# Attention and mixture-of-experts kernel on one core: the down projection of the leading shared blocks read as one 512-column product, its halves added by VectorE

## What is computed

```
x = x + layernorm(attention(layernorm(x)))
x = x + layernorm(ffn(layernorm(x)))

def ffn(hidden, gate_w, Wg, Wu, Wd, Sg, Su, Sd):
    flat_x = hidden.reshape(8192, 256)
    scores = softmax(flat_x @ gate_w.T).T                   # 16 experts
    topk_weight, topk_idx = top_k(scores, 1024)
    xg = flat_x[topk_idx]
    h = gelu(xg @ Wg.T) * (xg @ Wu.T)                       # 1024 hidden columns per expert
    eo = (h @ Wd.T) * topk_weight
    flat_out = zeros.at[topk_idx].add(eo)
    shared = (gelu(hidden @ Sg.T) * (hidden @ Su.T)) @ Sd.T # 512 hidden columns
    return flat_out + shared
```

## Time and profile before

| | |
|---|---|
| median of 3 runs | 1948.2 us (1948.04 to 1949.56) |
| the profiled execution's own time | 1948.25 us |
| its span, first to last instruction | 1946.2 us |
| TensorE busy | 1919.5 us, 99% |
| VectorE busy | 1368.9 us, 70% |
| ScalarE busy | 1036.9 us, 53% |
| mean granted TensorE clock | 0.996 |
| front blocks in the span | about 585 to 804 us |

### The profile page before, as it was taken

One profiled execution on the slowest core, in us unless ns is written; L12 is line 12 of the kernel. 1 busy time (PEld: TensorE's weight loads), 2 busy tenths in 40 slices (PEclk: granted clock), 3 DMA queues, 4 the chain that ended last, 5 costly groups with the idle time before them and its releaser, 6 DMA issues.

```text
span 1946.2 us, 29069 instructions
## 1 busy us (share of the span) xinstructions
PE 1919.5 (99%) x10608; PEld 1647.2 (85%) x10608; DVE 1368.9 (70%) x2619; ACT 1036.9 (53%) x1929; POOL 521.9 (27%) x611
## 2 busy tenths in 40 slices
PE   8999999999999999999999999999999999999996
PEld 6888888888888888888888888888888888888886
DVE  6777787777776888767677777656565756565647
ACT  5457576675655445445454544545454545455455
POOL 0031132033030000322432333243234323432146
PEclk9999999999999999999999999999999999999998
DMA  3113323324244111444434443444434443434566
GB/s 131 55 33 101 86 100 109 97 78 139 52 157 155 66 61 43 136 82 104 92 89 106 94 99 81 107 87 110 87 97 99 91 105 92 105 85 107 152 216 173
DMA packets 153338, 197.37 MB, mean 101 GB/s; under 512 B 104449, under 2 KB 121089, under 8 KB 145153
## 3 DMA queue, kind: packets, MB, share of 16 engines
q1 hardware_dynamic: 127824, 158.00, 26.1%
q0 software_dynamic: 25392, 37.77, 12.2%
HBM read 114.38 MB, written 59.34 MB: 89 GB/s over the span
## 4 chain that ended last, share of the span: by engine, by line
PE 66%; POOL 2%; DVE 1%; DMA 1%; issue 0%; ACT 0%; DVEq 0%; POOLq 0%
PE mo_psD L1637 12%; PE mo_psG L60 7%; PE mo_psU L60 7%; PE mo_psG L61 7%; PE mo_psG L62 7%; PE mo_psU L62 7%; PE mo_psU L61 7%; PE mo_psD L1642 6%; PE mo_psD L60 1%; PE mo_psD L61 1%; PE mo_psD L62 1%; DMA out_dram<-mo_F 1%; POOL mo_H_lo L2296 1%; PE mo_psX L1359 1%; POOL mo_rs L2306 0%
## 5 line engine op out<-in xcount | busy, mean ns | idle before, releaser
L1774 ACT ACTIVATE mo_HF<-mo_psG 128x512 f32<-128x512 f32 x320 | 191.8, 599 | 375.9 <-PE mo_psU L62 344.2
L2278 POOL DMA_INDIRECT ACC<-OUT,IDX x128 | 201.7, 1576 | 623.8 <-DVE OUT L2069 612.3
L1986 DVE TENSOR_TENSOR mo_HF<-mo_psU,mo_HF 128x512 f32<-128x512 f32 x320 | 220.4, 689 | 187.1 <-ACT mo_HF L1774 180.4
L1637 PE MATMUL mo_psD<-wd,mo_H_hi 128*128 128x512 f32 x1024 | 256.3, 392 | 0.3 <-DVE OUT L2069 0.3
L60 PE MATMUL mo_psG<-mo_XT_hi,wg_hi 128*128 128x512 f32 x640 | 253.7, 396 | 0.6 <-DVE mo_HF L1986 0.5
L60 PE MATMUL mo_psU<-mo_XT_hi,wu_hi 128*128 128x512 f32 x640 | 249.9, 390 | 0.0
L61 PE MATMUL mo_psG<-mo_XT_lo,wg_hi 128*128 128x512 f32 x640 | 249.8, 390 | 0.0
L62 PE MATMUL mo_psG<-mo_XT_hi,wg_lo 128*128 128x512 f32 x640 | 249.3, 390 | 0.0
L62 PE MATMUL mo_psU<-mo_XT_hi,wu_lo 128*128 128x512 f32 x640 | 249.0, 389 | 0.0
L61 PE MATMUL mo_psU<-mo_XT_lo,wu_hi 128*128 128x512 f32 x640 | 249.0, 389 | 0.0
L1637 PEld LDWEIGHTS mo_psD<-wd,mo_H_hi 128*128 128x128 f32 x1024 | 185.7, 188 | 35.2 <-DVE OUT L2069 0.5
(11 more groups left out here) (356 smaller groups left out, 3981.6 us busy)
## 6 DMA issues: line engine op xcount, KB each, us to landing
X1a<-wg_in SPq DMA_DIRECT2D x16, 1024.0 KB, 4.8
X1a<-wu_in SPq DMA_DIRECT2D x16, 1024.0 KB, 4.9
X1a<-wd_in SPq DMA_DIRECT2D x16, 1024.0 KB, 4.8
XN<-XG SPq DMA_DIRECT2D x8, 1088.0 KB, 4.1
X<-x_in SPq DMA_DIRECT2D x8, 1024.0 KB, 5.4
out_dram<-X SPq DMA_DIRECT2D x8, 1024.0 KB, 6.3
XN2T<-xn2T SPq DMA_DIRECT2D x8, 1024.0 KB, 5.1
X1a<-xt_in SPq DMA_DIRECT2D x7, 1024.0 KB
```

The lines of the kernel that those rows point to most:

```text
L1637: pe.matmul(psD[:, t % 2, :], hidden(b, it)[0][:, t * P:(t + 1) * P], wd_both[:, it, :, :].rearrange("p z d -> p (z d)"), start=(it == 0), ...
L1774: a.activation(HF[:, it % 2, :], psG[:, it % 2, :], ACT.Gelu).then_inc(s_gelu, 1)
L1986: v.tensor_tensor(HF[:, it % 2, :], psU[:, it % 2, :], HF[:, it % 2, :], ALU.mult).then_inc(s_mul, 1)
L2278: g.indirect_dma_start(out=io["ACC"], out_offset=bass.IndirectOffsetOnAxis(ap=c.IDX[:, n, 4 * tb + t:4 * tb + t + 1], axis=0), in_=OUT[:, ...
```

## The change

In the front blocks the three products of the down projection become two matmuls, as in the expert blocks. The down weights of the shared layer are laid out with high and low parts side by side per 128 hidden rows (`sd_both`, over the upper half of `wg1_hi` and the lower half of `wg1_lo`; the low part of the gate weights moves to the upper half of `wg1_lo`). TensorE issues four 512-column and four 256-column matmuls per tile. ScalarE's copy counts `s_half`, and VectorE adds the upper half of the bank to `OUT` and counts `s_ev`. These adds stand at the start of VectorE's `down(b)`: behind the steps, before the search's fifth count, the slots and the lists; in block 0 two of the four stand between the two parts of the layer norm's scale, in block 1 one before `v_scores` and three after it.

```
-        a.activation(self.c.sw[w][0].rearrange("p a n -> p (a n)"), self.raw_sh[w], ACT.Copy).then_inc(self.s_whi, 1)
+        hi = self.c.sw[w][0]
+        a.activation(hi, self.raw_sh[w].rearrange("p (a n) -> p a n", a=hi.shape[1]), ACT.Copy).then_inc(self.s_whi, 1)
...
-                    if is_e(b):
+                    if b < D0:
                         for it in range(n):
                             if t == 0:
                                 wait(pe, s_hhi, base[b] + it + 1)
                             pe.matmul(psD[:, t % 2, :], hidden(b, it)[0][:, t * P:(t + 1) * P],
-                                      wd_both[:, it, :, :].rearrange("p z d -> p (z d)"), start=(it == 0), stop=False)
+                                      both[:, it, :, :].rearrange("p z d -> p (z d)"), start=(it == 0), stop=False)
...
                         i = a.activation(OUT[:, t, :], psD[:, t % 2, 0:D], ACT.Copy, scale=scale)
-                        i.then_inc(s_ev if is_b(b) else s_half, 1)
+                        i.then_inc(s_half, 1)
...
+                def add_halves(ts):
+                    for t in ts:
+                        wait(v, s_half, 4 * b + t + 1)
+                        v.tensor_tensor(OUT[:, t, :], psD[:, t % 2, D:2 * D], OUT[:, t, :], ALU.add).then_inc(s_ev, 1)
+
                 if b == 0:
-                    tail.v_down0(v)
-                if b == 1:
+                    tail.v_down0(v, 0)
+                    add_halves(range(2))
+                    tail.v_down0(v, 1)
+                    add_halves(range(2, 4))
+                elif b == 1:
                     tail.v_shift(v, 1)
+                    add_halves(range(1))
                     tail.v_scores(v, 1)
+                    add_halves(range(1, 4))
+                elif is_b(b):
+                    add_halves(range(4))
                 if is_b(b):
                     if b < E0 - 1:
                         topk.vector_at(v, base[b + 1] + 1.5 - SHIFT)
...
-        c.sw = {"g": [cut(t, 0, KD) for t in c.wg1], "u": [cut(t, 0, KD) for t in c.wu1], "d": [cut(t, 1, I_SH // P) for t in c.wg1]}
+        c.sd_both = mem.over("sd", [P, I_SH // P, 2, D], F32R, "wg1_hi", 4 * KD * I_SH)
+        c.sw = {"g": [cut(t, z, KD) for z, t in enumerate(c.wg1)], "u": [cut(t, 0, KD) for t in c.wu1], "d": [c.sd_both[:, :, z, :] for z in (0, 1)]}
```

More of the change, by code:

```diff
@@ L218, in shared_hi @@
             a.wait_ge(self.s_w, 4)
-        a.activation(self.c.sw[w][0].rearrange("p a n -> p (a n)"), self.raw_sh[w], ACT.Copy).then_inc(self.s_whi, 1)
+        hi = self.c.sw[w][0]
+        a.activation(hi, self.raw_sh[w].rearrange("p (a n) -> p a n", a=hi.shape[1]), ACT.Copy).then_inc(self.s_whi, 1)
     def shared_lo(self, v, i):
-        hi, lo = (t.rearrange("p a n -> p (a n)") for t in self.c.sw["gud"[i]])
+        hi, lo = self.c.sw["gud"[i]]
         v.wait_ge(self.s_whi, i + 1)
-        v.tensor_tensor(lo, self.raw_sh["gud"[i]], hi.bitcast(F32), ALU.subtract)
+        v.tensor_tensor(lo, self.raw_sh["gud"[i]].rearrange("p (a n) -> p a n", a=hi.shape[1]), hi.bitcast(F32), ALU.subtract)
 def attention(nc, io, c):
@@ L1035, in v_end, with v_down0 @@
             self.v_stats(v, 1, x, range(4))
[L1037 to L1040, removed]
+    def v_down0(self, v, part):
+        if part == 0:
+            self.v_aggregate(v, 1)
+            v.drain()
+            layernorm_scale(v, 0, self.mv[1], self.ve[:, :], self.rs[1][:, :], self.shift[1][:, :], self.tmp[:, :], NT)
+            return
         layernorm_scale(v, 1, self.mv[1], self.ve[:, :], self.rs[1][:, :], self.shift[1][:, :], self.tmp[:, :], NT).then_inc(self.s_rx, 1)
@@ L1622, in down @@
                         wait(pe, s_wlo["d"], 4 * (expert(b)[0] + 1))
+                    both = wd_both
                 else:
-                    wd_hi, wd_lo = (bsw if is_b(b) else dsw)["d"]
+                    both, (wd_hi, wd_lo) = c.sd_both, dsw["d"]
                 for t in range(4):
@@ L1641, in down @@
                                 wait_lo(pe, b, it)
-                            i = pe.matmul(psD[:, t % 2, 0:D], hidden(b, it)[1][:, t * P:(t + 1) * P], wd[0][:, it, :],
+                            i = pe.matmul(psD[:, t % 2, 0:D], hidden(b, it)[1][:, t * P:(t + 1) * P], both[:, it, 0, :],
                                           start=False, stop=(it == n - 1))
@@ L2067, in down @@
                             topk.v_hival(v, AHEAD + h)
-                        wait(v, s_half, 4 * h + t + 1)
+                        wait(v, s_half, 4 * b + t + 1)
                         v.scalar_tensor_tensor(OUT[:, t, :], psD[:, t % 2, D:2 * D], TW[n % 2][:, 4 * tb + t:4 * tb + t + 1], OUT[:, t, :],
@@ L2379, in build @@
         cut = lambda t, i, k: t[:, :, :].rearrange("p a n -> p (a n)")[:, i * KD * I_SH:(i + 1) * KD * I_SH].rearrange("p (k n) -> p k n", k=k)
-        c.sw = {"g": [cut(t, 0, KD) for t in c.wg1], "u": [cut(t, 0, KD) for t in c.wu1], "d": [cut(t, 1, I_SH // P) for t in c.wg1]}
+        assert mem.place["wg1_lo"] == mem.place["wg1_hi"] + 2 * 4 * KD * I_SH
+        c.sd_both = mem.over("sd", [P, I_SH // P, 2, D], F32R, "wg1_hi", 4 * KD * I_SH)
+        c.sw = {"g": [cut(t, z, KD) for z, t in enumerate(c.wg1)], "u": [cut(t, 0, KD) for t in c.wu1], "d": [c.sd_both[:, :, z, :] for z in (0, 1)]}
         c.XR0 = mem.over("XR0", [P, KD, 512], F32, "wu1_hi", 4 * KD * I_SH)
```

## The result

The changed kernel takes 1995.8 us (median of 4 runs, 1992.7 to 1998.21), the kernel before 1948.2: ratio 1.0243, 95% interval 1.023 to 1.0255. Slower, as forecast, 5.8 us above the forecast and inside its range. The profiled execution has a span of 1996.2 us, 50.0 more than before, and a mean granted clock of 0.987 (0.996 before).

What follows compares the result with a forecast made beforehand. TensorE, busy 99% of the span, was taken to bound the kernel, so its waits count in full. 1948.2 + 33.1 net waits + 8.5 for the clock = 1990 us, range 1978 to 2001.

Steps and rivals of the forecast that it cites:

- The add stands behind the steps' work: Front blocks: tile 2 waits for tile 0's add, queued behind VectorE's step work; 3.1 us in each of blocks 2 to 7.
- An add costs 0.47 until TensorE moves: Each VectorE add in the front: 0.418 us by the nearest row, plus an estimated 0.05 for the semaphore.
- Net waits 33.1 us: TensorE's waits in the front blocks, 34.3 us in all, less the 1.2 us of matmul saving that remains.
- The fifth count is not late: Blocks 2 to 7: the count behind tile 3's add comes 0 to 0.2 us late a block; taken as 0.
- The matmuls' saving, 2.4 us: Front down tiles: 1.44 us becomes 1.39, 0.05 less on each of 48 tiles.
- The clock, 8.5 us, half of ten pauses: Front: ten long TensorE pauses, five assumed to bring half clock at 1.7 us each; bounds 0 and 17.
- Its records show no pause: Kernel before, 615.4 to 618.8: TensorE got half its clock although its records show no pause.
- A loop that pays every time: Cited from the Trainium skill: a wait before each burst of matmuls puts TensorE back to half clock every time.
- hidden: Rival: VectorE is in time, adds cost nothing and only the matmuls' saving shows; −2.4 us, 1945.8; chance 0.05.
- only the add's own time: Rival: tiles 2 and 3 of 12 blocks each wait 0.47, at most 11 us, about 1958; chance 0.05.
- every pause: Rival: all ten front pauses are answered by half clock, 17 us, giving 1998; chance 0.17.
- no pause: Rival: none of the ten front pauses is answered by half clock, giving 1981; chance 0.13.

Runs made afterwards that it cites:

- ghost: Changed kernel with the matmuls of before (new layout) and a one-column copy of OUT in place of each VectorE add; 1990.1 us, ratio 1.0221.
- mid: Changed kernel with the adds of tiles 0 and 1 moved directly ahead of VectorE's last step count, in blocks 2 to 7 only; 1981.1 us.
- early: Changed kernel, front blocks except 1 and 11: adds of tiles 0 and 1 inside VectorE's step before down, the others behind count, slots and lists; 1957.4 us.
- fill: Changed kernel with unread filler matmuls on TensorE ahead of tile 2's bank wait in blocks 0 and 2 to 10; 1985.3 and 1987.8 us.
- noadd: Changed kernel without VectorE's 48 adds, ScalarE's copy freeing the bank as before; 1949.1 us, ratio 1.0003.
- tail: Changed kernel with the adds of tiles 2 and 3 of blocks 2 to 10 moved behind the fifth count, slots and lists; 1988.3 us, ratio 1.0196.

## Why the prediction was right

- *TensorE's queue bounds, so a wait in it counts in full.* Right: the expert stage shifts by a constant 48.6.
- *The add stands behind the steps' work.* Right, block by block, but for block 1. Blocks 2 to 7: forecast 3.1, TensorE starts tile 2 3.0 later relative to tile 0. Block 0: 5.1, measured 5.07. Block 8: 1.4 and 2.3, measured 1.29 and 2.13. Block 9: 2.7, measured 2.54. Block 10: 1.0 and 3.3, measured 1.00 and 3.60. Block 1 was costed at 0, at most 0.5; its tile 3 waited 0.63. Ghost, mid and early change only the place in the queue and the wait follows it.
- *An add costs 0.47 until TensorE moves.* 0.48 in block 6.
- *Net waits 33.1 us.* 33.7 to 35.4 (fill).
- *The fifth count is not late.* Right: such waits come to 0.2 us in the changed kernel.
- *The matmuls' saving, 2.4 us.* Mis-sized: noadd shows no measurable difference, and by its tiles 0.02 to 0.03 each, about 1 us. The price of the eight 512-column matmuls of an expert was taken for groups of four.
- *The clock, 8.5 us, half of ten pauses.* Mis-sized, though inside its bounds. In the profiled run six of the ten pauses named have half clock in or behind them, and so has the first one of block 8, which I had not counted; in blocks 0 and 10 it lasts 6.7 us instead of 3.3, in part while TensorE stands still. It cost 11.6 to 13.3 us. That the pauses cause most of it is shown by fill. "Half" was a middle between two bounds and not worked out from anything; that six of ten came so near it is luck. Which pauses are followed is not known: of the equal ones of blocks 2 to 7 it is two of six in the changed kernel, three of six in tail and in ghost, and others each time.
- *"Its records show no pause"* before the fall at 615.4 in the kernel before. True, but I did not look at what they do show, thirty-two matmuls of 16 columns:

```profile
611.19 3.75 PE L900 MATMUL mo_psX<-gw,xn2T 128*128 128x16 f32 x32
```

  The changed kernel has the same ones from 619.36 on and falls at 623; fill has them too and stays at full clock. So a pause is not the only thing that half clock can stand behind, and no run here shows what brings this one.
- *A loop that pays every time.* The loop of the Trainium skill ("TensorE: Matmul & The Clock Gate", HAM oscillation) has waits of about 3 to 5 us, and each one is paid for. This case agrees at that length, in blocks 0 and 10 (5.1 and 3.6 us). Below it, it goes either way: four of the six pauses of 2.9 us in the changed kernel were not paid for, and one of 1.3 us was.
- *Outside the sum.* In the profiled run 1.7 us more came from the fall in attention and 1.4 from behind the last matmul. The four timings lie 5.5 us apart, and how the median's 47.6 us divide is not recorded.

Of the rivals, "hidden" and "only the add's own time" are refuted, by ghost and the waits above; "every pause" (1998) and "no pause" (1981) lie on either side of what was measured.

## What to carry to other kernels

When a buffer's release moves from one engine to another, what counts is how far behind that engine's queue is at that moment, not how long its instruction takes: 0.42 us of add cost 3 us a block, and a one-column copy in its place almost as much. Look for the last instruction ahead of it in program order, and compare its end with the start of the work that wants the buffer. And a pause of 1 to 5 us in front of dense matmuls is to be priced as a range: nothing, one stretch of half clock behind it (1.7 us here), or two. The runs here do not let one say beforehand which pauses will pay.

## What the runs showed of the hardware

- Equal pauses of 2.9 us before dense matmuls were followed by half clock in two blocks of six in the changed kernel and in three of six in tail, where two of the stretches were 6.8 us long; equal pauses of 2.6 us in three of six in ghost; pauses of 1.2 us in mid in none of six. In the profile of fill no pause filled with matmuls nobody reads was followed by it.
- A pause of 1.29 us behind six one-column matmuls (block 8) was followed by half clock in the changed kernel, in mid and in tail, one of 1.02 us there in ghost.
- In block 0's pause of 5.07 us the half clock was granted 2.6 us before its end and lasted 6.8 us.
- Four 512-column matmuls behind 256-column ones took 0.2325 us each (noadd), eight of them 0.2275.
